# Linear attention plus an fp8 linear layer on one core: inter product in 64x32 tiles, output products in K's bank, VectorE's step reordered

## The reference, cut to what matters

```python
xn  = layernorm(x)                                  # x: 4 sequences x 2048 tokens x 512
q, k, v = heads(xn @ Wq.T + bq), heads(xn @ Wk.T + bk), heads(xn @ Wv.T + bv)   # 64 heads of 8
q, k = softmax(exp(beta) * q), softmax(exp(beta) * k)       # over the 8 elements of a head
kv  = cumsum(einsum('zsD,zsd->zsDd', k, v), axis=1)         # causal: a running 8x8 state per head
kn  = cumsum(k, axis=1)
out = einsum('zsD,zsDd->zsd', q, kv) / sum(q * kn, axis=-1)
attn = out @ Wo.T + bo
ffn  = fp8_e4m3(clip(xn / in_scale)) * in_scale @ (w_fp8 * w_scale).T + bias
return x + attn + ffn
```

## Time and profile before

| | |
|---|---|
| median of 3 runs | 1249.07 us (1248.55 to 1250.06) |
| span of the profiled execution | 1248.2 us |
| what lies between the span and the median | 0.87 us |
| mean granted TensorE clock | 0.982 |
| TensorE matmul busy | 1174.9 us, 94% |
| VectorE busy | 977.9 us, 78% |
| ScalarE busy | 744.9 us, 60% |
| GpSimd busy | 321.6 us, 26% |

### The profile page before, as it was taken

One profiled execution on the slowest core, in us unless ns is written; L12 is line 12 of the kernel. 1 busy time (PEld: TensorE's weight loads), 2 busy tenths in 40 slices (PEclk: granted clock), 3 DMA queues, 4 the chain that ended last, 5 costly groups with the idle time before them and its releaser, 6 DMA issues.

```text
span 1248.2 us, 60447 instructions
## 1 busy us (share of the span) xinstructions
PE 1174.9 (94%) x26082; PEld 679.2 (54%) x26082; DVE 977.9 (78%) x1968; ACT 744.9 (60%) x1177; POOL 321.6 (26%) x590
## 2 busy tenths in 40 slices
PE   1459999999999999999999999999999999999996
PEld 1235555555555555555555555555555555555553
DVE  4567887888788788878878887788788778878873
ACT  0456656665666666566666656666665666566652
POOL 3122222322222232222223232222323232222310
PEclk9689999999999999999999999999999999999999
DMA  9022334334334433433333343343343433333331
GB/s 234 21 59 70 81 90 89 78 80 91 82 82 87 89 80 79 90 86 80 85 89 82 77 90 89 78 84 91 81 79 91 84 83 81 91 82 81 72 73 46
DMA packets 156483, 104.64 MB, mean 84 GB/s; under 512 B 111968, under 2 KB 128480, under 8 KB 156256
## 3 DMA queue, kind: packets, MB, share of 16 engines
q1 hardware_dynamic: 155536, 99.76, 35.7%
q10 hardware_dynamic: 720, 1.31, 0.4%
HBM read 40.20 MB, written 16.78 MB: 46 GB/s over the span
## 4 chain that ended last, share of the span: by engine, by line
PE 92%; issue 3%; DVE 2%; DMA 1%; ACT 1%; POOL 1%; SPq 0%; POOLq 0%; DVEq 0%; ACTq 0%
PE s_ps L900 10%; PE a_ps L917 7%; PE a_ps L1018 6%; PE a_ps L999 6%; PE k_ps L873 5%; PE vo_ps L975 5%; PE vo_ps L873 5%; PE k_ps L877 5%; PE k_ps L875 5%; PE vo_ps L884 4%; PE vo_ps L888 4%; PE vo_ps L886 4%; PE vo_ps L877 4%; PE vo_ps L875 4%; PE q_ps L877 4%; PE q_ps L873 4%
## 5 line engine op out<-in xcount | busy, mean ns | idle before, releaser
L521 ACT ACTIVATE q_heads<-qT,cst 128x512 f32<-128x512 f32 x256 | 163.9, 711 | 88.2 <-DVE qT L769 88.2
L407 POOL TENSOR_TENSOR y_sum<-y,y_magic 128x512 f32<-128x512 f32 x64 | 81.4, 1272 | 433.0 <-DVE y_magic L629 433.0
L506 ACT ACTIVATE w_own<-kT,cst 128x512 f32<-128x512 f32 x128 | 85.5, 715 | 166.7 <-DVE kT L711 166.7
L530 ACT ACTIVATE st_seqs<-st_run,cst 128x576 f32<-128x576 f32 x252 | 181.5, 797 | 0.5 <-DVE st_run L665 0.5
L671 DVE TENSOR_TENSOR att<-s_ps,cst 128x512 f32<-128x512 f32 x256 | 163.8, 682 | 0.4 <-PE s_ps L900 0.4
L400 POOL TENSOR_TENSOR x_split<-xn,x_split 128x512 f16<-128x512 f32 x64 | 74.1, 1158 | 291.6 <-ACT x_split L462 284.3
L900 PE MATMUL s_ps<-q_heads,w_own 64*64 64x128 f32 x4096 | 141.3, 275 | 0.6 <-DVE att L671 0.6
L900 PEld LDWEIGHTS s_ps<-q_heads,w_own 64*64 64x64 f32 x4096 | 110.4, 132 | 54.3 <-issue 54.2
L462 ACT ACTIVATE x_split<-xn 128x512 f16<-128x512 f32 x64 | 40.3, 630 | 126.7 <-DVE xn L618 126.7
L873 PE MATMUL k_ps<-w_hi,xT 128*128 128x512 f16 x256 | 98.9, 386 | 17.0 <-DMA xT<-x_split 12.3
L727 DVE TENSOR_TENSOR vp<-vo_ps,vp 128x512 f32<-128x512 f32 x64 | 44.3, 692 | 86.3 <-PE vo_ps L877 86.3
(11 more groups left out here) (136 smaller groups left out, 2287.8 us busy)
## 6 DMA issues: line engine op xcount, KB each, us to landing
v_groups<-vp SPq DMA_DIRECT2D x512, 36.0 KB, 3.1
x_in<-L_attn_x SPq DMA_DIRECT2D x64, 256.0 KB
x_res<-L_attn_x SPq DMA_DIRECT2D x64, 256.0 KB
out<-o_sb SPq DMA_DIRECT2D x64, 256.0 KB
w_own<-L_attn_Wk SPq DMA_DIRECT2D x1, 1024.0 KB, 13.0
w_own<-L_attn_Wq SPq DMA_DIRECT2D x1, 1024.0 KB, 15.0
w_own<-L_attn_Wv SPq DMA_DIRECT2D x1, 1024.0 KB, 16.5
att<-L_ffn_weight_fp SPq DMA_DIRECT2D x1, 1024.0 KB, 18.1
```

The source lines that it names most:

```text
L506: last = sc.activation(k_pairs[:, i.parity, :, c, :], kT[:, :, :], ACT.Copy, scale=pair_mask[:, c:c + 1])
L521: last = sc.activation(q_heads[:, i.parity, :, j, :], qT[:, i.parity, :, :], ACT.Copy, scale=head_mask[:, j:j + 1])
L530: last = sc.activation(st_seqs[:, i.parity, :, :, b, :].rearrange("p g j w -> p (g j) w"), st_run[:, :, :, :].rearrange("p g j w -> p (g j ...
```

## The change

The inter product is cut by pairs of sequences. Each product takes 64 partitions of `qT` (two sequences) as weights and streams `st_pairs`, in which the state stands twice (once per member of a pair): 4 heads x 2 sequences x 9 = 72 columns. There are 32 products in place of 16. The columns of `a_ps` are laid out anew, so that the bank is chosen by the pair of sequences; the intra product and `normalise_attention` address the new layout, with the same shapes of instructions. ScalarE makes two masked copies of the state in place of four.

The fp8 layer's and output's products add up in `k_ps`. ScalarE seeds it with the output bias after the exponential of K, and with K's bias for the next iteration after the seed of `q_ps`, when `o_ready` says that VectorE has read the sum. V keeps `vo_ps` alone and waits for `vp_ready` of the step before, not for `o_ready`.

On VectorE `magic` moves ahead of `al`; the transpose of the queries moves behind `mask_state` 1 and `output`; `add_state` moves behind `statistics` and `variances`. On TensorE the parts of `body` become functions that are called in the same order.

```diff
-        st_seqs = sb("st_seqs", [P, 2, G, J, SEQS, VW])
-        den_rec = sb("den_rec", [P, 2, G // 2 * SEQS])
+        st_pairs = sb("st_pairs", [P, 2, G, J, SP, VW])
+        den_rec = sb("den_rec", [P, 2, G * SP])
...
-        a_view = a_halves[:, :, 0:G // 2 * GW]
-        a_rows = a_view.rearrange("p n (l r) -> p n l r", l=GP)
+        a_view = a_halves[:, :, 0:G * SP * VW]
+        a_rows = a_view.rearrange("p n (h l j r) -> p n h l j r", h=2, l=GP, j=J)
...
             def body(i, last_weights=None, fold=False):          # ScalarE
-                t = i - 2
-                if t.exists():
-                    if (t + 1).exists():
-                        act.wait_ge(vp_ready, (t + 2).n)
-                    else:
-                        act.wait_ge(o_ready, t.n)
...
-                    sc.activation(vo_ps[:, :], bias[:, 3, :], ACT.Copy, scale=out_up[:, :])\
-                        .then_inc(oseed_ready, 1)
+                d = i - 2
                 if (i + 1).exists():
                     high_input(i + 1)
...
                     sc.activation(k_e[:, i.parity, :], k_shift[:, :], ACT.Exp, scale=k_exp_scale[:, :])\
                         .then_inc(ke_ready, 1)
-                    if (i + 1).exists():
-                        sc.activation(k_ps[:, :], bias[:, MK, :], ACT.Copy).then_inc(kseed_ready, 1)
+                if d.exists():
+                    if not i.exists():
+                        act.wait_ge(o_ready, d.n)
...
+                    sc.activation(k_ps[:, :], bias[:, 3, :], ACT.Copy, scale=out_up[:, :])\
+                        .then_inc(oseed_ready, 1)
...
                     if (i + 1).exists():
                         sc.activation(q_ps[:, :], bias[:, MQ, :], ACT.Copy).then_inc(qseed_ready, 1)
+                        if d.exists():
+                            act.wait_ge(o_ready, (d + 1).n)
+                        sc.activation(k_ps[:, :], bias[:, MK, :], ACT.Copy).then_inc(kseed_ready, 1)
...
-                    for b in range(SEQS):
-                        last = sc.activation(st_seqs[:, i.parity, :, :, b, :].rearrange("p g j w -> p (g j) w"),
+                    for c in range(SP):
+                        last = sc.activation(st_pairs[:, i.parity, :, :, c, :].rearrange("p g j w -> p (g j) w"),
                                              st_run[:, :, :, :].rearrange("p g j w -> p (g j) w"),
-                                             ACT.Copy, scale=seq_mask[:, b:b + 1])
+                                             ACT.Copy, scale=pair_mask[:, c:c + 1])
...
             def body(i, last_weights=None, fold=False):          # VectorE
...
+                if t.exists() and i.exists():
+                    mask_state(t, 0)
+                if (i + 1).exists():
+                    magic(i + 1)
+                if d.exists():
+                    split_low(d)
...
                 if i.exists():
                     key_sums(i)
+                if i.exists():
                     shift(i, q_ps, q_done, q_max, qmax_ready, q_shift, qshift_ready, qe_ready)
-                if (i + 1).exists():
-                    magic(i + 1)
                 if t.exists():
                     mask_scores(t, 2)
                     mask_scores(t, 3)
-                if i.exists():
-                    dve.wait_ge(qe_ready, (i + 1).n)
...
-                    v.transpose(qT[:, i.parity].rearrange("p g s -> p (g s)"), q_e[:, :]).then_inc(qT_ready, 1)
                 if t.exists() and i.exists():
                     mask_state(t, 1)
...
-                if (i - 2).exists():
-                    output(i - 2)
-                if t.exists() and i.exists():
-                    add_state(t)
+                if d.exists():
+                    output(d)
+                if i.exists():
+                    turn_queries(i)
                 if (i + 3).exists():
                     statistics(i + 3)
                 if i.parity == 0 and (i + PAIR).exists():
                     variances(i + PAIR)
+                if t.exists() and i.exists():
+                    add_state(t)
                 if i.exists():
                     scale_values(i)
...
+            def values(i, fold):                                  # TensorE
...
+                if i.after(1):
+                    pe.wait_ge(vp_ready, i.n)
+                project(vo_ps, i, MV, seeded=False).then_inc(v_done, 1)
...
+            def quantised(t, low_part):
...
+                    last = mm(k_ps[:, :], xq[:, t.slot, c, :], w_hi[:, MF, c, :], start=False,
+                              stop=False, skip_group_check=True)
...
-                    for n in range(2):
-                        for gp in range(GP):
-                            for u in range(J):
-                                g = G // 2 * n + GP * u + gp
-                                mm(a_rows[TOK * u:TOK * (u + 1), n, gp, :], qT[:, t.parity, g, :],
-                                   st_seqs[:, t.parity, g].rearrange("p j b w -> p (j b w)"),
-                                   start=(gp == 0), stop=False, skip_group_check=True)
+                for h in range(2):
+                    for gp in range(GP):
+                        for u in range(J):
+                            g = G // 2 * h + GP * u + gp
+                            for n in range(SEQS // SP):
+                                rows = slice(SP * TOK * n, SP * TOK * (n + 1))
+                                mm(a_rows[TOK * u:TOK * (u + 1), n, h, gp].rearrange("p j r -> p (j r)"),
+                                   qT[rows, t.parity, g, :],
+                                   st_pairs[rows, t.parity, g].rearrange("p j c w -> p (j c w)"),
+                                   start=(h == 0 and gp == 0), stop=False, skip_group_check=True)
...
-                if i.exists():
-                    if fold:
-                        pe.wait_ge(fold_ready, 1)
-                    if (i - 2).exists():
-                        pe.wait_ge(o_ready, (i - 1).n)
-                    project(vo_ps, i, MV, seeded=False).then_inc(v_done, 1)
```

More of the change, by code:

```diff
@@ L892, in scores @@
             def scores(t, half):
+                if half == 0:
+                    pe.wait_ge(kpairs_ready, (t + 1).n)
+                    pe.wait_ge(qheads_ready, (t + 1).n)
+                    if t.after(1):
+                        pe.wait_ge(att_ready, t.n * 4)
+                else:
+                    pe.wait_ge(att_ready, t.n * 4 + 2)
                 pe.sem_inc(pe_waited, 1)
@@ new lines, in turn_attention @@
+            def turn_attention(t):
+                pe.wait_ge(an_ready, (t + 1).n)
+                if t.after(1):
+                    pe.wait_ge(al_ready, t.n)
+                else:
+                    pe.wait_ge(bvl_ready, 1)
+                for b in range(SEQS):
+                    last = transpose(t_ps[:, :].rearrange("p (j b s) -> p b j s", b=SEQS, s=TOK)[:, b],
+                                     a_n[:, b, :, :].rearrange("p g d -> p (g d)"), ident)
+                last.then_inc(aT_done, 1)
@@ new lines, in quantised @@
+            def quantised(t, low_part):
+                pe.wait_ge(xq_turned, (t + 1).n * 16)
+                pe.wait_ge(oseed_ready, (t + 1).n)
+                for c in range(KC):
+                    last = mm(k_ps[:, :], xq[:, t.slot, c, :], w_hi[:, MF, c, :], start=False,
+                              stop=False, skip_group_check=True)
+                    if low_part:
+                        last = mm(k_ps[:, :], xq[:, t.slot, c, :], w_lo[:, MF, c, :], start=False,
+                                  stop=False, skip_group_check=True)
+                last.then_inc(f_done, 1)
@@ new lines, in intra @@
+            def intra(t, h):
+                pe.wait_ge(att_ready, t.n * 4 + 2 * h + 2)
+                if h == 0:
+                    for b in range(SEQS):
+                        pe.wait_ge(v_moved[t.parity][b], (t + 2).half * 16 * GP)
+                    pe.sem_inc(pe_waited, 1)
+                for n in range(SEQS // SP):
+                    for j in range(J):
+                        for u in range(J):
+                            last = mm(a_rows[TOK * u:TOK * (u + 1), n, h, :, j, :],
+                                      att[:, n, J * h + u, j, :],
+                                      v_groups[:, t.parity, :, n, J * h + u, j, :], start=False, stop=True,
+                                      skip_group_check=True)
+                if h == 1:
+                    last.then_inc(a_done, 1)
@@ L921, in body @@
             def body(i, low_part=True, last_weights=None, fold=False):
+                t, d = i - 1, i - 2
                 if i.exists():
[L923 to L926 removed]
+                    keys(i)
                 if t.exists():
[L928 to L931 removed]
@@ L934, in body @@
                         state(t, 0)
-                t = i - 2
-                if t.exists():
-                    pe.wait_ge(an_ready, (t + 1).n)
-                    if t.after(1):
-                        pe.wait_ge(al_ready, t.n)
```

(14 more changed lines are left out.)

140 lines of the change are left out of this document (59 added, 81 removed).

## The result

The changed kernel takes 1218.95 us (median of 4 runs, 1218.42 to 1221.45) against 1249.57 us for the kernel before on the same chip (1248.55 to 1251.76): ratio 0.9753, 95% interval 0.9736 to 0.9770, so 2.5% or some 31 us faster. The profile is of the execution of 1221.45 us, the slowest of the four and 2.5 us above their median; its span is 1219.6 us.

What follows compares the result with a forecast made beforehand. TensorE was taken as the bound, busy 94% of the span. From 1248.2 us of span, 26.9 (inter product) and 11 (mask wait) come off: 1210.3 us, as a median 1211.2 us, range 1202 to 1226.

Steps and rivals of the forecast that it cites:

- The inter product: On TensorE, 32 products of 72 columns over eight tiles: slot from 1.12 to 0.70 us, gaining 26.9 us.
- The wait for the mask: Inter product waiting for VectorE's mask_state 1: 0.19 us a step goes, 11 us, bounds 7.1 to 12 us.
- The banks: V alone in vo_ps, fp8 and output products in k_ps: no gain of its own, K's seed 3 us early.
- part 1: The inter product's recut into 32 products of 72 columns on TensorE, worth 0.42 us a step.
- ScalarE: Two of four state copies go, half of 2.89 us: worth nothing by itself, pays for the later seed.
- VectorE's end of the step: VectorE from the read of the sum on: the moved transpose fits, with 0.3 us over.
- The signs: Expected in the profile: inter product entry 0.65 to 0.8 us, step 17.5 us, TensorE above 93% busy, ScalarE's copies some 90 us.
- Four at a time: Rival: row halves and column strips don't combine on TensorE, slot 1.15 us, kernel 1238 us; chance 0.09.
- VectorE as the bound: Rival: VectorE's 14.8 us of work and small waits fill a 17.5 us step, kernel 1230 us; chance 0.05.
- The cost per instruction: Rival: a 64x32 instruction costs by issue and weight load, inter product 2.06 us, kernel 1298 us; chance 0.08.
- The floor of 25 ns: Skill's rule against the change: 64 inter product instructions take 1.60 us, kernel 1269 us; within a rival's chance of 0.08.

Runs made afterwards that it cites:

- e6: Changed kernel with the 32 inter products reordered, all of one row half ahead of the other: 1231.43 us, ratio 0.9836 to the kernel before.
- e9: Changed kernel with the inter product's loops turned round, four column strips of one row half first within each wave of eight: 1220.6 us, ratio 0.9761.
- e10: Changed kernel with all 32 inter products issued a second time: 1300.69 us, ratio 1.0395 to the kernel before.
- e5: Kernel before with VectorE's new order of calls and nothing else: 1240.1 us, ratio 0.9918 to the kernel before.
- e7: Changed kernel with only the transpose of the queries moved back ahead of mask_state 1: 1219.82 us, ratio 0.9763 to the kernel before.
- e12: Changed kernel with only magic moved back behind the shift of the queries: 1219.9 us, ratio 0.9761 to the kernel before.
- e4: Changed kernel with VectorE's whole order of calls as before: 1236.74 us, ratio 0.9894 to the kernel before.
- e3: Changed kernel with fp8 and output products back in vo_ps, V waiting for o_ready again, K's seed free of that wait: 1228.6 us, ratio 0.9818.
- e2: Kernel before with the inter product's new tiles, layout and two state copies, nothing else: 1236.84 us, ratio 0.9875 to the kernel before.
- e8: Changed kernel with two further masked state copies on ScalarE into a tile nobody reads: 1219.18 us, ratio 0.9763 to the kernel before.
- e11: Changed kernel with V's products moved ahead of the inter product: 1278.22 us, ratio 1.022 to the kernel before.

## Why the prediction was right

The forecast was 1211.2 us, -38 us, at a step of 17.52 us; measured are 1218.95 us, -31 us, at 17.63 to 17.71. The mechanism held in all parts that the sum rests on: the tiles, the wait for the mask and the separate bank. One term was mis-sized, and its 0.81 us lie just outside the 0.56 to 0.80 us that I had given it.

- **The inter product.** I took 0.70 us for its slot and said why: half of the state has as many instructions of the same load, and takes 0.69 us. Measured are 0.81 to 0.82 us. 64 x 0.11 = 7 us is nearly the whole of the 7.7 us by which the forecast is off. e6 shows that the gain comes from both row halves at work together, e9 that their order in a wave doesn't matter. The start times show where the nearest row misled. The first 32 instructions are alike: the 32nd starts at 0.26 us in the inter product and at 0.27 us in the state. Then the inter product has a hole of 0.06 us, and its last 31 start 10.8 ns apart, the state's 9.3 ns apart, so that the last one starts at 0.66 against 0.57 us. In e10 a further 64 of them cost 10.3 ns each. Why the later ones come more slowly wasn't tried.
- **The wait for the mask.** Forecast 11 us, e5 gives 10.2. Its margin of 0.9 us is in the profile: the mask ends 0.91 us ahead of the inter product. I added up both moves; e7 and e12 show that either is enough by itself. What the prediction left out is that the wait grows with the shorter step: e4 loses 17.6 us. It made no difference to the sum, because the wait goes either way.
- **The banks.** "It lets part 1 through" holds: with the bank undone 8 of the tiles' 18 us are lost (e3). "No gain of its own" was not run; with the tiles and the old order the bank gave none (e2 against e4).
- **ScalarE** was worth nothing (e8), and K's seed came 3.3 us early, where I had worked out 3.
- **VectorE's end of the step.** It fits, as forecast, in the step with `variances` too: `scale_values` follows `add_state` at once at 612.20, and 0.49 us of idle are left ahead of the reciprocals. One edge was missed. The square root on GpSimd comes too late in every second step: VectorE waits 0.67 us for it ahead of `normalise` (L618). GpSimd starts right after `variances` and takes until 615.37 us; its first small operation lasts 0.74 us here, where it lasted 0.19 in the kernel before. In the new order it runs beside `add_state` (611.53 to 612.29 us); whether that is the reason was not tried. The wait costs nothing: in e7 it doesn't occur after the run's first, and the time is the same.

```profile
611.60 0.74 POOL L385 TENSOR_TENSOR newton<-guess 128x2 f32<-128x2 f32 x1 [6.62 <-DVE guess L609]
```

- **The signs.** The inter product's entry at 0.81 us and the steps at 17.63 to 17.71 us are both a little over what I had named (0.65 to 0.8, and 17.5 throughout). The others came as said: no idle ahead of the inter product, TensorE 95% busy, 0.95 us of idle ahead of `output`, no wait for K's seed, 94 us for the state copies.
- **The rivals.** Four at a time: the slot would be 0.99 us as in e6 (I had put it at 1.15), and it is 0.81. VectorE as the bound: TensorE is busy 200.00 of 200 us. The cost per instruction: the slot would have had to pass 1.31 us. The floor of 25 ns between matmuls that the Trainium skill states (TensorE: Matmul & The Clock Gate, section Wait, 56ns, not 53.3ns?) doesn't hold for these tiles: 64 instructions in 0.81 us are 12.7 ns each, and in e10 64 more cost 10.3 ns each.

## What to carry to other kernels

When an engine is busy 99% of the time, shorten its work, but look first at which wait on another engine is level with it: the wait for the mask was worth 10 us alone and 18 once the products were shorter, and the separate bank nothing while VectorE had its old order, 8 us with the new one. A reserve can be read as idle time on the other engine just ahead of its next wait for the bound one. Don't put long runs of small products back to back on the strength of a sum of slots: the same instructions in another place cost 58 us, because TensorE ran out of instructions. The page's queue of the kind "instruction" is where to look when TensorE waits and no semaphore is named.

## What the runs showed of the hardware

- Eight 64x32 fp32 tiles, with a PSUM bank per row half, work side by side: 64 instructions of 72 columns take 0.81 us, and 0.99 us when only one row half is in reach for half of the slot (e6). In the first half of the slot eight start every 62 ns, in e6's last part four. The order within the eight is free (e9).
- TensorE can run out of instructions. They come in DMA packets of 256 (16 packets more for 4096 instructions more), and in e11 and e10 TensorE stood still for up to 2.5 us, 53 times in all, each time until 1.2 to 1.6 us after the end of such a packet. The Trainium skill (Runtime: NRT & Kernel Launch, section Instruction fetch mechanics) says that instructions are refilled in blocks of 256 and that crossing a block is mostly hidden. The first agrees with the counts here. The second holds in the changed kernel, where the intra product's group lost 0.4 us in all, and not in e11, where the same group lost 39.9 us.
- A standstill can cost the clock as well. After four of e11's (2.0 to 2.5 us long) the granted clock went to the 1.2 GHz level, which made each of those steps 1.8 to 1.9 us longer.
